# Other tick places for all pieces of a two-layer attention kernel, and layer 3's last transposes behind the next score

## The chip, the core and the metric

One core of one Trainium2 chip runs the whole kernel. The metric is device time in microseconds (us), taken from the first to the last instruction of the program with what lies around it.

## What is computed

32 batch elements, each a matrix x of 256 tokens by 256 features, go through four layers, cut here to what matters:

```python
# layer 0: conditioned norm over the whole matrix, twice, with two products
o = silu(scale * norm_all(x) + shift) @ W_in + b_in
x = silu(scale * norm_all(o) + shift) @ W_out + b_out + x
# layer 1: attention with 16 heads of 16, a bias of its own for each element and head, a mask
h = ln(x) * (1 + ada_scale) + ada_shift
s = einsum(q / 4, k) + attention_bias ; s[mask] = -inf
x = h + softmax(s) @ v @ Wo + bo
x = x + gelu2(ln(x) * g2 + beta2) @ W1 ... @ W2     # 256 -> 1024 -> 256
# layer 2: a small stencil on the matrix, coefficients from two grids
x = maximum(x + dt * (-grad(A x) + 0.5 * grad2(B x)), 0)
# layer 3: causal attention of 16 heads, then the 256 -> 1024 -> 256 block
x1 = x + causal_attention(ln(x)) @ Wo + bo
x2 = x1 + gelu(ln(x1) * gamma2 + beta2 ...) @ W2 + b2
out = x + gate * (x2 - x)
```

## The kernel before

The kernel is one long program without loops on the chip: the loops are unrolled when it is written. Work is cut into pieces with names (`score0`, `t4`, `w3` and so on), and time into ticks. Each element takes a PERIOD of 64 ticks. The layer-1 attention of element b starts at tick 64 b and its layer-3 attention at 64 b + 160 (`begin`, `S3`). An attention has 8 units of two heads, one each 4 ticks; in a steady period PE alternates between the 8 units of layer 1 of one element and the 8 of layer 3 of the element two before. A unit is called by its number, 0 to 7. The table `P` gives each piece its place in ticks from the begin of its element's layer (pieces named in `LATE` count from layer 3's), and `OWN` gives other places for the first two elements (0, 1) and the last two (-2, -1). `place` looks a place up, and from the places a table of what is due at each tick is made.

Each engine's program is written by one pass over the ticks: at each tick, first the attention pieces and then the others in the order in which the code has them. So a place only decides the order of instructions on their own engine; what makes an engine wait are semaphores. A smaller place is an earlier position in the queue, not an earlier time. Numbers that change without passing another piece of the same engine change nothing.

The queues and the pieces that the prediction speaks of:

- SyncE (SP) issues all loads. `ld_bt` (L396) loads the bias tile of a layer-1 unit into one of four BT buffers, after `v_bias` says that bias1 of the unit four before has been done. `stack` (L407 for Q, L411 for K) copies, for a pair of units, the rows of Q and K that its two scores need into Qs and Ks: three DMAs for Q and six for K, into one of two buffer sets. `ld_x`, `ld_xn` (L383), `ld_ab`, `ld_mask` (L390) load the element's inputs once each.
- TensorE (PE): `score0`, `score1` (L1191, wait for the stack's DMAs, `d_st`), `flip` (L1199, transposes of the exponentials), `pv` (L1217, L1218). For the tail of layer 3: `c3` (L1163, four transposes of the attention's result CX), `o3` (L1156, product with Wo), `t4` (L1163, four transposes of the normalised rows TC), `w3` (L1171, four groups of products with TN, the transposed rows), `w4`. Others are `wout` (L1156), `n2_ones` (L1263), `v3` (L1156) and so on.
- VectorE (DVE): `bias0`, `bias1` (L786, adds the bias tile and takes the row maximum), `low` (L794), `pvn` (L801 to L807, makes CX), `v3_out` (L867, reads v3's bank), `m4` (L945, and the statistics behind it), `f1` (L883), `n1_scale`, `n2_sum`, `n2_center`, `s_re`, `s_w`.
- ScalarE (ACT): `exp` (L990), `high` (L996), `c3_out` (L1088, copies c3's bank to TC), `m4_norm` (L1005, makes TC), `t4_out` (L1011, copies t4's bank to TN), `v1_mid`, `v1_hi`, `q1_out`, `t3_out`.
- GpSimd (POOL): `mask_add` (L497, adds the mask to the bias tile), `mask`, `y3`, `x1_bo`, `m1_b`, `q3_lo`, `k3_lo`.

c3, o3, t4, w3 of layer 3 and v3 of the next element share one PSUM bank, `bT_`, except for the last element. Therefore c3 of element b also waits for `v3_out` of element b + 1:

```python
for b in at(t, "c3"):
    ...
        T.wait_ge(v_v[3], b + 2)
```

The stack of unit 6 stands behind `ld_bt` of unit 7 in SP's queue. On PE, in a steady period around unit 6 of layer 1 of element 10, the order is: flips of unit 3, score1 of 5, pv of 2, `t4` of element 7, score0 of 6, flips of 4, `w3` group 0.

Of the kernel before, what the change touches and what calls it, by code (L numbers as in the profile page):

```python
# [42 lines left out]
def begin(layer, b):  # L43
# [6 lines left out]
    "score0": -2, "score1": 0, "bias0": 1, "bias1": 3, "exp0": 3, "exp1": 6, "flip0": 7, "flip1": 7,  # L50
    "high0": 8, "high1": 8, "low0": 10, "low1": 10, "pv0": 12, "pv1": 12, "pvn": 15,
    "ld_bt": -14, "mask_add": -9, "stack": -10,
    "ld_x": -103, "ld_xn": -34, "ld_ab": -34, "ld_mask": -109, "mask": -25,

# [7 lines left out]

# [2 lines left out]
    "s_pm": 74, "s_b": 82, "s_r": 74, "s_rp": 79, "s_re": 91, "s_ha": 83, "s_w": 91, "s_ab": 92, "s_row": 92,  # L65
    "s_mm": 95, "s_f": 104,

    "ld_w1": -24, "ld_sten": -46, "ld_w3": -277, "coefs": -21,

    "film_a": -72, "film": -62, "adas": -57, "scr": -48,  # L70

# [28 lines left out]
    },  # L100
# [5 lines left out]
        "s_b": 91, "s_r": 85, "s_rp": 86, "s_ha": 93, "s_w": 93, "s_ab": 93, "s_row": 93, "s_f": 98, "m3": -54,  # L106
# [4 lines left out]
    },  # L111
# [1329 lines left out]
```

## Time and profile before

| what | us |
|---|---|
| median of 3 runs | 2738.4 (2736.6 to 2738.7) |
| the profiled execution | 2738.3 |
| its span | 2737.0 |

Busy time in the span: PE 2599.0 (95%), ACT 2338.8 (85%), DVE 2221.9 (81%), PE's weight loads 2214.0 (81%, beside its matmuls), POOL 1674.0 (61%). The granted TensorE clock has a mean of 0.984 of full speed. The chain that ended last is 71% PE and 13% ACT. An engine's row in the timeline gives start, duration, line, operation, out<-in, the number of instructions in the row, and in brackets how long the engine had stood idle before it and what released it.

### The profile page before, as it was taken

To read this page: it belongs to the slowest core of one execution; us is meant where nothing else is said; L and a number is where in the kernel's file an instruction comes from. 1 tells how busy PE (TensorE), PEld (TensorE's weight loads), DVE (VectorE), ACT (ScalarE), POOL (GpSimd) and SP (SyncE) were. 2 spreads that over 40 slices of the span, in tenths; PEclk is the share of its full clock that TensorE was granted. 3 is DMA by queue.
4 is the path that set the end of the run, shared out by engine and by line. 5 is a ranking of instruction groups with operands and counts; after the bars stand their busy time and mean duration, and the time that the engine had idled before them with its cause. 6 is when DMAs were issued, how large, how long until landed. Compare 5 with 4: busy or idle time off the path is not lost.

```text
span 2737.0 us, 62626 instructions
## 1 busy us (share of the span) xinstructions
PE 2599.0 (95%) x20072; PEld 2214.0 (81%) x20072; DVE 2221.9 (81%) x7925; ACT 2338.8 (85%) x5285; POOL 1674.0 (61%) x1742
## 2 busy tenths in 40 slices
PE   8888999999999999999999999999999999999987
PEld 7766888888888888888888888888888888888776
DVE  5668888888888888888888888888888888888753
ACT  1567899999999999998999989999998998999865
POOL 2666666766667675666666566666666666765431
PEclk8988999999999999999999999999999999999999
DMA  6433343333333333333333333343333333333211
GB/s 230 130 96 102 91 118 108 116 102 113 96 103 115 109 114 103 110 98 101 114 112 112 103 108 101 98 119 108 113 97 114 101 100 116 109 105 102 63 31 29
DMA packets 176549, 287.96 MB, mean 105 GB/s; under 512 B 45856, under 2 KB 99104, under 8 KB 175840
## 3 DMA queue, kind: packets, MB, share of 16 engines
q1 hardware_dynamic: 176224, 283.97, 35.2%
q8 instruction: 162, 2.65, 0.4%
q14 instruction: 163, 1.34, 0.2%
HBM read 174.64 MB, written 8.45 MB: 67 GB/s over the span
## 4 chain that ended last, share of the span: by engine, by line
PE 71%; ACT 13%; issue 4%; SPq 4%; DVE 3%; POOL 2%; DMA 2%; ACTq 0%; DVEq 0%; POOLq 0%
PE bank L1171 15%; PE bank L1178 14%; PE bank L1199 10%; PE bank L1156 9%; PE bank L1148 8%; PE bank L1191 5%; ACT PB L990 3%; PE bank L1163 3%; SPq L411 2%; ACT PH L996 2%; PE bank L1306 2%; ACT BB L1011 2%; PE bank L1217 2%; PE bank L1218 2%; ACT AA L1011 2%
## 5 line engine op out<-in xcount | busy, mean ns | idle before, releaser
L990 ACT ACTIVATE PB<-PB,mx 128x256 f32<-128x256 f32 (+1 forms) x2048 | 834.6, 475 | 6.0 <-DVE mx L786 5.2
L794 DVE TENSOR_TENSOR PO<-bank,PH 128x384 f16<-128x384 f32 (+1 forms) x1024 | 589.4, 616 | 247.5 <-ACT PH L996 244.4
L497 POOL TENSOR_TENSOR BT<-BT,MN 128x1024 f32<-128x1024 f32 x256 | 545.9, 2137 | 174.2 <-DMA BT<-in_bias 173.4
L996 ACT ACTIVATE PH<-bank 128x384 f16<-128x384 f32 (+1 forms) x1024 | 499.0, 538 | 127.7 <-PE bank L1199 127.2
L1191 PE MATMUL bank<-Ks,Qs 96*128 96x512 f32 (+1 forms) x1024 | 519.1, 510 | 19.5 <-DMA Ks<-KU 11.9
L1199 PE MATMUL bank<-ident,PB 128*128 128x128 f32 x3584 | 484.8, 275 | 8.5 <-ACT PB L990 4.5
L1199 PEld LDWEIGHTS bank<-ident,PB 128*128 128x128 f32 x3584 | 421.2, 142 | 46.8 <-ACT PB L990 12.3
L786 DVE CUSTOM_DVE_ANT_0 PB<-bank,BT 128x256 f32<-128x256 f32 x1024 | 386.7, 416 | 37.6 <-PE bank L1191 36.2
L786 DVE CUSTOM_DVE_ANT_0 PB<-bank,caus 128x128 f32<-128x128 f32 (+1 forms) x1024 | 321.0, 351 | 22.9 <-PE bank L1191 22.5
L1217 PEld LDWEIGHTS bank<-VP,PH 128*128 128x128 f16 x3584 | 204.0, 96 | 119.2 <-issue 93.5
L1171 PE MATMUL bank<-TN,Wf 128*128 128x256 f32 x1024 | 253.9, 391 | 16.6 <-ACT BB L1011 11.4
L1171 PE MATMUL bank<-MB,Wf 128*128 128x256 f32 x1024 | 251.9, 389 | 14.2 <-ACT AA L1011 13.0
L1217 PE MATMUL bank<-VP,PH 128*128 128x49 bf16 x3584 | 257.5, 186 | 7.8 <-DVE CX L807 2.7
L1218 PE MATMUL bank<-VP,PO 128*128 128x49 bf16 x3584 | 249.7, 184 | 0.0
L1178 PE MATMUL bank<-Wf,BB 128*128 128x256 f32 x1024 | 244.8, 384 | 0.7 <-ACT BB L1000 0.7
L1178 PE MATMUL bank<-Wf,AA 128*128 128x256 f32 x1024 | 239.3, 381 | 1.6 <-ACT AA L1076 1.6
L1191 PEld LDWEIGHTS bank<-Ks,Qs 96*128 96x128 f32 x1024 | 195.1, 191 | 41.2 <-DMA Ks<-KU 16.0
L1171 PEld LDWEIGHTS bank<-TN,Wf 128*128 128x128 f32 x1024 | 184.9, 190 | 51.5 <-ACT BB L1011 21.0
L1171 PEld LDWEIGHTS bank<-MB,Wf 128*128 128x128 f32 x1024 | 184.2, 190 | 45.7 <-ACT AA L1011 24.0
L1178 PEld LDWEIGHTS bank<-Wf,AA 128*128 128x128 f32 x1024 | 189.4, 190 | 27.0 <-issue 2.1
L1218 PEld LDWEIGHTS bank<-VP,PO 128*128 128x128 f16 x3584 | 207.9, 97 | 0.7
L1178 PEld LDWEIGHTS bank<-Wf,BB 128*128 128x128 f32 x1024 | 185.2, 190 | 22.2 <-issue 1.0
(225 smaller groups left out, 5208.8 us busy)
## 6 DMA issues: line engine op xcount, KB each, us to landing
BT<-in_bias SPq DMA_DIRECT2D x256, 512.0 KB, 3.9
Qs<-QH SPq DMA_DIRECT2D x512, 64.0 KB, 2.4
Ks<-KH SPq DMA_DIRECT2D x1024, 32.0 KB, 2.0
Qs<-QU SPq DMA_DIRECT2D x256, 64.0 KB, 2.5
Ks<-KU SPq DMA_DIRECT2D x512, 32.0 KB, 2.0
XT<-in_xT SPq DMA_DIRECT2D x32, 256.0 KB, 2.9
X<-in_x SPq DMA_DIRECT2D x32, 256.0 KB, 2.9
AB<-ada_rows SPq DMA_DIRECT2D x32, 256.0 KB, 3.6
```

The lines of the kernel that those rows point to most:

```text
L497: G.op.tensor_tensor(v2(BT[k % 4]), v2(BT[k % 4]), MN[:, :].unsqueeze(1).broadcast_to([128, 2, 512]), ALU.add).then_inc(g_bt, 1)
L786: V.op.tensor_tensor_reduce(PB[(2 * D + q) % 6][:, h * 256:h * 256 + w], bS[q][:, h * w:h * w + w], plus, -1.0, 3.0e38, ALU.add, ALU.min, ...
L794: V.op.tensor_tensor(PO[i][:, 0:w], bP[h][:, 0:w], PH[i][:, 0:w], ALU.subtract).then_inc(v_low, 1)
L990: S.op.activation(o, o, ACT.Exp, scale=-1.0, bias=mx[u.layer][:, c:c + 1]).then_inc(a_exp, 1)
L996: S.op.activation(PH[i][:, 0:w], bP[h][:, 0:w], ACT.Copy).then_inc(a_high, 1)
L1156: last = T.op.matmul(half(ps, m), x[:, k * 256 + m * 128:k * 256 + m * 128 + 128], Wf[:, a + k * 256:a + k * 256 + 256], start=(k == 0), s ...
L1171: last = T.op.matmul(half(ps, f), Wf[:, c:c + 128], half(x, d), start=(d == 0), stop=(d == 1))
L1178: last = T.op.matmul(half(ps, q), x[:, f * 256 + q * 128:f * 256 + q * 128 + 128], Wf[:, c:c + 256], start=(g == 0 and f == 0 and q == 0), ...
L1191: T.op.matmul(bS[q][:, 0:2 * w].rearrange("p (h k) -> p h k", h=2), Qs[i][0:96, et * 256 + q * 128:et * 256 + q * 128 + 128], k2[:, :, 0:w ...
L1199: last = T.op.transpose(bP[h][:, c * 128:c * 128 + 128], PB[(2 * u.D + q) % 6][:, h * 256 + k * 128:h * 256 + k * 128 + 128], ident[:, :])
L1217: T.op.matmul(bV[:, o:o + 49], PH[i][:, c * 128:c * 128 + 128], vv, start=(n == 0), stop=False)
L1218: last = T.op.matmul(bV[:, o:o + 49], PO[i][:, c * 128:c * 128 + 128], vv, start=False, stop=(n == len(ks) - 1))
```

## The change

Only numbers in `P` and `OWN` change; each piece issues the same instructions as before. In steady periods `t4` moves from tick 53 to 54 of layer 3, which puts it behind `score0` of unit 6 of the layer-1 attention that runs beside it. `c3` moves from 45 to 43, ahead of score1 and the pv pair of the tick before. The rest of the table changes by small amounts, with `ld_xn`, `ld_mask`, `mask`, `ld_bt` and `stack` among them, and the places of the first two and the last two elements by larger ones. The diff, with `OWN` cut to lines that hold pieces spoken of:

```diff
--- before.py
+++ after.py
@@ -47,32 +47,32 @@
 
 
 P = {
-    "score0": -2, "score1": 0, "bias0": 1, "bias1": 3, "exp0": 3, "exp1": 6, "flip0": 7, "flip1": 7,
+    "score0": -2, "score1": 0, "bias0": 0, "bias1": 3, "exp0": 3, "exp1": 6, "flip0": 7, "flip1": 7,
     "high0": 8, "high1": 8, "low0": 10, "low1": 10, "pv0": 12, "pv1": 12, "pvn": 15,
-    "ld_bt": -14, "mask_add": -9, "stack": -10,
-    "ld_x": -103, "ld_xn": -34, "ld_ab": -34, "ld_mask": -109, "mask": -25,
-
-    "n1_stats": -81, "n1_ones": -68, "n1_sum": -66, "n1_center": -65, "n1_rstd": -66, "n1_scale": -60,
+    "ld_bt": -9, "mask_add": -7, "stack": -3,
+    "ld_x": -102, "ld_xn": -60, "ld_ab": -35, "ld_mask": -118, "mask": -7,
+
+    "n1_stats": -82, "n1_ones": -68, "n1_sum": -66, "n1_center": -65, "n1_rstd": -66, "n1_scale": -63,
     "n1_tanh": -58, "n1_gate": -56, "win": -49, "win_out": -45,
-    "n2_stats": -39, "n2_ones": -39, "n2_sum": -38, "n2_center": -36, "n2_rstd": -36, "n2_scale": -34,
-    "n2_tanh": -31, "n2_gate": -31, "xb": -33, "wout": -30, "x1": -28, "x1_rstd": -25, "x1_norm": -25,
-    "ada": -23, "t1": -21, "t1_out": -20, "x1_bo": -3, "q1": -19, "q1_out": -17, "q1_lo": -13,
-    "k1": -17, "k1_out": -13, "k1_lo": -10, "v1": -13, "v1_out": -9, "v1_hi": -5, "v1_sub": 7, "v1_mid": 8,
-    "v1_lo": 10,
-
-    "c1": 44, "c1_out": 45, "o1": 45, "m1": 47, "m1_rstd": 47, "m1_norm": 53, "m1_b": 71, "t2": 54, "t2_out": 54,
-    "w1": 57, "w1_out": 58, "w1_gelu": 66, "w2": 68, "f1": 74,
-    "s_pm": 74, "s_b": 82, "s_r": 74, "s_rp": 79, "s_re": 91, "s_ha": 83, "s_w": 91, "s_ab": 92, "s_row": 92,
-    "s_mm": 95, "s_f": 104,
-
-    "ld_w1": -24, "ld_sten": -46, "ld_w3": -277, "coefs": -21,
-
-    "film_a": -72, "film": -62, "adas": -57, "scr": -48,
-
-    "m3": -41, "m3_rstd": -41, "m3_norm": -35, "t3": -34, "t3_out": -33, "y3": -25, "q3": -30, "q3_out": -25,
-    "q3_lo": -24, "k3": -25, "k3_out": -24, "k3_lo": -14, "v3": -22, "v3_out": -19, "v3_hi": -4, "v3_sub": 1,
-    "v3_mid": 9, "v3_lo": 10, "c3": 45, "c3_out": 45, "o3": 46, "m4": 49, "m4_rstd": 50, "m4_norm": 52, "m4_b": 65,
-    "t4": 53, "t4_out": 54, "w3": 55, "w3_out": 57, "w3_gelu": 67, "w4": 69, "out": 75, "st_out": 77,
+    "n2_stats": -40, "n2_ones": -39, "n2_sum": -36, "n2_center": -36, "n2_rstd": -35, "n2_scale": -34,
+    "n2_tanh": -31, "n2_gate": -31, "xb": -30, "wout": -30, "x1": -29, "x1_rstd": -26, "x1_norm": -25,
+    "ada": -23, "t1": -21, "t1_out": -20, "x1_bo": -18, "q1": -19, "q1_out": -18, "q1_lo": -14,
+    "k1": -17, "k1_out": -13, "k1_lo": -8, "v1": -13, "v1_out": -9, "v1_hi": -4, "v1_sub": -3, "v1_mid": 3,
+    "v1_lo": 9,
+
+    "c1": 44, "c1_out": 45, "o1": 45, "m1": 47, "m1_rstd": 48, "m1_norm": 52, "m1_b": 64, "t2": 54, "t2_out": 54,
+    "w1": 57, "w1_out": 58, "w1_gelu": 66, "w2": 68, "f1": 73,
+    "s_pm": 74, "s_b": 81, "s_r": 74, "s_rp": 79, "s_re": 88, "s_ha": 87, "s_w": 89, "s_ab": 91, "s_row": 93,
+    "s_mm": 95, "s_f": 103,
+
+    "ld_w1": -32, "ld_sten": -56, "ld_w3": -164, "coefs": -31,
+
+    "film_a": -81, "film": -65, "adas": -62, "scr": -60,
+
+    "m3": -39, "m3_rstd": -37, "m3_norm": -36, "t3": -34, "t3_out": -34, "y3": -26, "q3": -30, "q3_out": -25,
+    "q3_lo": -18, "k3": -25, "k3_out": -24, "k3_lo": -18, "v3": -22, "v3_out": -19, "v3_hi": -3, "v3_sub": 1,
+    "v3_mid": 11, "v3_lo": 13, "c3": 43, "c3_out": 45, "o3": 46, "m4": 48, "m4_rstd": 52, "m4_norm": 52, "m4_b": 72,
+    "t4": 54, "t4_out": 54, "w3": 55, "w3_out": 57, "w3_gelu": 67, "w4": 69, "out": 75, "st_out": 79,
 }
 
 LATE = {
@@ -90,54 +90,56 @@
 OWN = {
     -2: {
...
-        "y3": -29, "q3": -41, "q3_out": -37, "q3_lo": -32, "k3": -37, "k3_out": -36, "k3_lo": -30, "v3": -29,
-        "v3_out": -22, "v3_hi": -22, "v3_sub": -21, "v3_mid": -16, "v3_lo": -14, "c3": 51, "c3_out": 112, "o3": 121,
-        "m4": 141, "m4_rstd": 145, "m4_norm": 150, "m4_b": 282, "t4": 153, "t4_out": 155, "w3": 159, "w3_out": 162,
+        "y3": -42, "q3": -45, "q3_out": -41, "q3_lo": -31, "k3": -38, "k3_out": -38, "k3_lo": -23, "v3": -37,
+        "v3_out": -23, "v3_hi": -19, "v3_sub": -19, "v3_mid": -17, "v3_lo": -16, "c3": 36, "c3_out": 137, "o3": 151,
+        "m4": 157, "m4_rstd": 167, "m4_norm": 171, "m4_b": 268, "t4": 175, "t4_out": 177, "w3": 196, "w3_out": 197,
...
     -1: {
...
-        "pvn_3": 110, "stack_3": 611, "c1": 43, "c1_out": 46, "o1": 47, "m1": 50, "m1_rstd": 51, "m1_norm": 55,
+        "pv1_3": 114, "pvn_3": 118, "stack_3": 608, "c1": 45, "o1": 47, "m1": 51, "m1_rstd": 52, "m1_norm": 56,
-        "t4": 578, "t4_out": 635, "w3": 638, "w3_out": 742, "w3_gelu": 910, "w4": 653, "out": 885, "st_out": 1135,
+        "m4_b": 575, "t4": 545, "t4_out": 574, "w3": 659, "w3_out": 769, "w3_gelu": 901, "w4": 733, "out": 965,
...
     0: {
...
-        "n2_rstd": -39, "n2_scale": -39, "n2_tanh": -39, "n2_gate": -38, "xb": -67, "wout": -33, "x1": -33,
+        "n1_gate": -54, "win": -51, "win_out": -50, "n2_stats": -48, "n2_ones": -48, "n2_sum": -44, "n2_center": -42,
-        "v3_sub": 0, "v3_mid": 4, "c3": 44, "m4": 47, "m4_rstd": 47, "t4": 54, "w3_gelu": 66, "out": 76, "st_out": 84,
+        "v3_mid": 2, "v3_lo": 10, "c3_out": 44, "m4": 49, "out": 76, "st_out": 89,
...
     1: {
...
-        "mask_add_1": 1, "stack_1": -13, "stack_3": -9, "ld_x": -72, "ld_xn": -57, "ld_ab": -28, "ld_mask": -62,
-        "n2_tanh": -33, "n2_gate": -33, "xb": -29, "x1_rstd": -26, "x1_norm": -24, "ada": -21, "t1": -18,
+        "mask_add_1": -5, "stack_1": -11, "stack_3": -5, "ld_x": -64, "ld_xn": -43, "ld_ab": -44, "ld_mask": -88,
+        "win_out": -53, "n2_stats": -52, "n2_ones": -51, "n2_sum": -49, "n2_center": -43, "n2_rstd": -49,
+        "n2_scale": -40, "n2_tanh": -37, "n2_gate": -35, "xb": -40, "wout": -35, "x1": -32, "x1_rstd": -30,
...
```

## Rows read from the trace of the kernel before

**Rows 1.** The page's busy times by engine.

```profile
PE 2599.0 (95%) x20072; PEld 2214.0 (81%) x20072; DVE 2221.9 (81%) x7925; ACT 2338.8 (85%) x5285; POOL 1674.0 (61%) x1742
```

**Rows 2.** Stretches: length; PE, PEld, DVE, ACT, POOL busy; clock; DMA share; GB/s.

```profile
859.40:939.40 80.00, 77.87 (x614) 66.59 (x613) 68.46 (x248) 72.78 (x166) 52.21 (x55) 1.00 0.36 107
1259.20:1340.80 81.60, 78.09 (x614) 66.69 (x613) 68.75 (x248) 72.92 (x166) 51.93 (x55) 1.00 0.36 105
```

**Rows 3.** PE's waits, 400 to 2400 us: us, times, longest.

```profile
PE bank L1163 <- ACT TC L1005: 20.6, 25, 1.1
PE bank L1156 <- ACT TC L1088: 11.3, 25, 0.5
...
PE bank L1191 <- DMA Ks<-KU: 2.7, 6, 1.4
```

**Rows 4.** Timeline of DVE, one steady period: v3_out, second half of bias1.

```profile
856.71 0.69 DVE L867 TENSOR_TENSOR HB<-bank,rows 128x512 f32<-128x512 f32 x1
...
858.99 0.42 DVE L786 CUSTOM_DVE_ANT_0 PB<-bank,BT 128x256 f32<-128x256 f32 x1
```

**Rows 5.** Timeline of SP, same period: ld_bt 7, first and last of the stack.

```profile
859.44 0.33 SPq L396 DMA_DIRECT2D BT<-in_bias  x1
859.82 0.57 SPq L407 DMA_DIRECT2D Qs<-QH  x1
...
864.29 1.23 SPq L411 DMA_DIRECT2D Ks<-KU  x2
```

**Rows 6.** All DMAs into Ks, from the view of that tile.

```profile
DMA to landing us min/median/max: 1.9/2.0/4.1
```

**Rows 7.** Timeline of PE, same period: c3, o3, t4, score0 of 6, flips, w3.

```profile
857.70 0.63 PE L1163 MATMUL bank<-ident,CX 128*128 128x128 f32 x4
...
859.02 1.99 PE L1156 MATMUL bank<-Wf,TC 128*128 128x256 f32 x8 [0.45 <-ACT TC L1088]
...
867.18 0.65 PE L1163 MATMUL bank<-ident,TC 128*128 128x128 f32 x4 [0.78 <-ACT TC L1005]
867.59 0.48 PE L1191 MATMUL bank<-Ks,Qs 96*128 96x512 f32 x1
867.90 1.04 PE L1199 MATMUL bank<-ident,PB 128*128 128x128 f32 x8
868.94 1.99 PE L1171 MATMUL bank<-TN,Wf 128*128 128x256 f32 x8
```

**Rows 8.** Timeline of ACT, same period: m4_norm and t4_out.

```profile
866.04 1.08 ACT L1005 ACTIVATE TC<-Y,smt 128x256 f32<-128x256 f32 x2
...
867.87 1.02 ACT L1011 ACTIVATE TN<-bank,cols 128x256 f32<-128x256 f32 x2
```

**Rows 9.** Timeline of SP, period from 1259.20: a long issue in the stack.

```profile
1260.24 2.80 SPq L407 DMA_DIRECT2D Qs<-QU  x1
1263.09 0.59 SPq L407 DMA_DIRECT2D Qs<-QH  x1
```

**Rows 10.** Timeline of PE, the same late period: score0 of 6, then w3.

```profile
1269.01 0.51 PE L1191 MATMUL bank<-Ks,Qs 96*128 96x512 f32 x1 [1.36 <-DMA Ks<-KU]
...
1270.22 1.03 PE L1171 MATMUL bank<-TN,Wf 128*128 128x256 f32 x4
```

**Rows 11.** The page's DMA queues: instructions (packets, MB, share).

```profile
q8 instruction: 162, 2.65, 0.4%
```

**Rows 12.** The page's groups: busy, mean ns, idle before and its releaser.

```profile
L794 DVE TENSOR_TENSOR PO<-bank,PH 128x384 f16<-128x384 f32 (+1 forms) x1024 | 589.4, 616 | 247.5 <-ACT PH L996 244.4
L497 POOL TENSOR_TENSOR BT<-BT,MN 128x1024 f32<-128x1024 f32 x256 | 545.9, 2137 | 174.2 <-DMA BT<-in_bias 173.4
L996 ACT ACTIVATE PH<-bank 128x384 f16<-128x384 f32 (+1 forms) x1024 | 499.0, 538 | 127.7 <-PE bank L1199 127.2
```

**Rows 13.** Timeline of PE near the start: the largest wait.

```profile
166.32 2.93 PE L1156 MATMUL bank<-Wf,FU 128*128 128x256 f32 x6 [4.12 <-DVE FU L758]
```

**Rows 14.** Timeline of PE near the end: w3 of element 30, a score.

```profile
2671.50 1.99 PE L1171 MATMUL bank<-TN,Wf 128*128 128x256 f32 x8 [1.11 <-ACT TN L1011]
...
2693.18 0.39 PE L1191 MATMUL bank<-Ks,Qs 96*128 96x256 f32 x1 [1.20 <-DMA Ks<-KU]
```

More of the change, by code:

```diff
@@ L92 @@
     -2: {
[7 rows of a table removed]
[7 rows of a table added]
     },
     -1: {
[4 rows of a table removed]
-        "s_b": 91, "s_r": 85, "s_rp": 86, "s_ha": 93, "s_w": 93, "s_ab": 93, "s_row": 93, "s_f": 98, "m3": -54,
[4 rows of a table removed]
-    },
[11 rows of a table removed]
-        "s_b": 88, "s_r": 88, "s_rp": 90, "s_re": 95, "s_ha": 95, "s_w": 96, "s_ab": 97, "s_row": 98, "s_mm": 100,
[3 rows of a table removed]
-    },
-    1: {
-        "score0_1": 1, "score1_1": 3, "bias0_1": 3, "exp0_1": 6, "flip0_1": 11, "flip1_1": 11, "high0_1": 12,
-        "high1_1": 12, "low0_1": 14, "low0_3": 9, "low1_1": 14, "pv0_1": 15, "pv1_1": 15, "pvn_1": 18, "ld_bt_1": -16,
-        "mask_add_1": 1, "stack_1": -13, "stack_3": -9, "ld_x": -72, "ld_xn": -57, "ld_ab": -28, "ld_mask": -62,
[6 rows of a table removed]
-        "s_r": 80, "s_rp": 88, "s_ha": 97, "s_w": 100, "s_ab": 101, "s_row": 106, "s_mm": 106, "s_f": 108,
-        "m3_rstd": -35, "y3": 0, "q3_lo": -25, "k3_out": -23, "k3_lo": -7, "v3_hi": -19, "v3_sub": -18, "v3_mid": -14,
-        "v3_lo": -10, "m4_b": 71, "out": 77,
[4 rows of a table added]
+        "s_b": 94, "s_r": 87, "s_rp": 88, "s_re": 94, "s_ha": 94, "s_w": 94, "s_ab": 94, "s_row": 94, "s_f": 101,
[4 rows of a table added]
+        "st_out": 1032,
+    },
+    0: {
+        "score0_1": 1, "score1_1": 3, "bias0_1": 4, "bias1_1": 5, "exp0_1": 5, "exp1_1": 7, "flip0_1": 8,
+        "flip1_1": 8, "high1_1": 10, "low0_1": 11, "low1_1": 11, "ld_bt_1": -3, "mask_add_1": 1, "stack_1": 4,
+        "stack_3": -1, "ld_x": -322, "ld_xn": -41, "ld_ab": -56, "ld_mask": -57, "mask": -39, "n1_stats": -219,
[7 rows of a table added]
+        "s_r": 82, "s_rp": 83, "s_re": 93, "s_ha": 96, "s_w": 97, "s_ab": 97, "s_row": 100, "s_mm": 100, "s_f": 108,
[3 rows of a table added]
+    },
+    1: {
+        "score1_1": -1, "bias0_1": 2, "bias0_3": 1, "exp0_1": 6, "flip0_1": 8, "flip1_1": 8, "high0_1": 11,
+        "high1_1": 12, "low0_1": 12, "low1_1": 12, "pv0_1": 14, "pv1_1": 14, "pvn_1": 18, "ld_bt_1": -18,
+        "mask_add_1": -5, "stack_1": -11, "stack_3": -5, "ld_x": -64, "ld_xn": -43, "ld_ab": -44, "ld_mask": -88,
[7 rows of a table added]
+        "s_w": 97, "s_ab": 99, "s_row": 104, "s_mm": 104, "s_f": 107, "m3": -51, "y3": 22, "q3_lo": -21, "k3_lo": -17,
+        "v3_out": -21, "v3_hi": -14, "v3_sub": -13, "v3_mid": -5, "v3_lo": 12, "m4_b": 68, "w3_gelu": 66, "out": 77,
+        "st_out": 83,
     },
```

49 rows, old and new, of the table OWN are left out of this document.

## The prediction

> **What bounds the kernel now.** I read the page first for the busiest engine: TensorE (PE) is busy for 2599.0 of 2737.0 us, and no other engine comes near [rows 1]. So the time is PE's own work plus the holes in it, and only an edit that changes the holes can change the time, since no instruction is added or removed. The table by stretches says where the holes are: a normal period of one batch element (80 us) has 77.87 us of PE, while one that starts at 1259.20 takes 81.6 us with 78.09 us of it [rows 2]. About 28 of the 32 periods (elements 3 to 30) are of this kind. Then PE's waits between 400 and 2400 us, 25 periods: two waits come once in every period, 20.6 us in all ahead of t4 (L1163, for m4_norm on ACT) and 11.3 us ahead of o3 (L1156, for c3_out on ACT); third, a wait in some periods only, 2.7 us in 6 times, where a score (L1191) waits for the DMAs of its stack [rows 3]. The change moves exactly t4 and c3, so these are read in the timeline.
>
> Times in a period are told from A, the end of bias1 of unit 3 of the layer-1 element on DVE, 858.99 + 0.42 = 859.41 in the period shown [rows 4]. On it hangs SP: ld_bt of unit 7 waits for that bias1 (it goes out at 859.44), and the nine DMAs of the stack of units 6 and 7 stand behind it on SP, 859.82 to 865.52 [rows 5]. From issue to landing such a DMA takes 1.9/2.0/4.1 us (min, median, max) [rows 6]; the last one goes out at about 864.9, so the stack lands at 866.94, which is A+7.52 and what the landing events show in 12 of the 28 periods within 0.05 us.
>
> In the period shown PE has finished the pv pair of unit 2 at 866.40, waits 0.78 us for m4_norm, does t4 at 867.18, score0 of unit 6 at 867.59, eight flips from 867.90, and w3.0 at 868.94 [rows 7]. m4_norm ends at 866.04 + 1.08 = 867.12, t4_out at 867.87 + 1.02 = 868.89 [rows 8], so w3.0 starts right at the end of t4_out. It is important that the score did not wait: it came 0.65 us after its landing, because the wait of t4 had covered it.
>
> **The change, part one: t4 behind score0 of unit 6 (P: 53 to 54).** The thought behind such an order is that the score fills t4's wait. The score can't: PE is free at 866.40 but the stack lands only at 866.94, so the wait becomes one for the stack and stays 0.58 of the 0.78 us. From then on, with the differences of the starts in the rows: score0 at landing + 0.04 (866.98), t4 0.32 later (867.30; the step from score to the next transpose is 867.90 - 867.59 = 0.31), t4 lasts 0.66, t4_out starts 0.05 behind and lasts 1.02, and w3.0, which multiplies what t4_out wrote, starts 0.05 behind that: landing + 2.13 = 869.07 instead of 868.94. That is +0.13 us: t4 itself has been made 0.12 later, and PE, which now finishes the flips about 0.2 us early, waits for t4_out in front of w3.0. Everything behind w3.0 on PE (scores of unit 6 and 7, n2_ones, w3.1 to w3.3) waits with it, and there is nothing in the row of PE to win it back before the next A, as the period has only some 2 us of holes.
>
> The price is higher where the stack is late, and it is late often. In the period from 1259.20 one Q DMA of the stack takes 2.80 us to issue instead of 0.59 [rows 9], the landing comes at A+9.75, and the score waits 1.36 us; t4 was already done under the wait and w3.0 follows at 1270.22, which is landing + 1.25 [rows 10]. With t4 behind the score, t4 and t4_out come after the landing in a row, and w3.0 comes at landing + 2.13: +0.88 us. Such long issues coincide with packets of the instruction queue (162 in the execution, about one each 17 us [rows 11]), so they walk through the period. The Trainium skill ("Runtime: NRT & Kernel Launch", section Instruction fetch mechanics) says that crossing a block of instructions is mostly hidden; by it all stacks would land at A+7.52 and the price would be the small one in every period. The trace disagrees with 2.80 us where 0.59 is usual.
>
> I worked the same two sums for each of the 28 periods from its own rows: w3.0 of before against the later of landing + 2.13 and its PE order. Nine periods have landings from A+8.05 to A+9.75 that give 0.74 to 0.88 each (7.7 us together), six, most with landings from A+7.7 to A+8.0, give 0.3 to 0.6 (2.65 us), thirteen give -0.1 to 0.17 (0.9 us). Sum **+11.3 us**. If no stack were late it would be 28 x 0.13 = +3.6, if all rest were as bad as the nine, 28 x 0.6 = +17; I take 11.3, since the number of SP instructions in a period stays and only two loads move past the stack, so the late issues come as often as before. I assume that a delay of w3.0 reaches the end of the period 1:1: the period of 1259.20 is 1.65 us longer than 79.96, and its w3.0 is 1.47 us later than usual (A+11.01 for A+9.54).
>
> **Part two: c3 ahead of score1 and the pv pair (45 to 43).** In before c3 (857.70) lets c3_out end at 858.97 and o3 waits 0.45 us for it to 859.02 [rows 7]. With c3 earlier the 0.45 looks free, up to 28 x 0.45 = 12.6 us. But c3's bank is the one that v3 of the next element used, and c3 waits for its reader v3_out on DVE, which ends at 856.71 + 0.69 = 857.40 [rows 4]. So c3 starts at about 857.44 instead of 857.70, now holding back score1's successors and the pv pair behind it, which takes the place of the wait: c3_out ends 0.26 earlier, and o3 follows the c3, pv pair and score0 issued behind it (1.27 us in all) at about 858.99. Gain 0.03 us a period, and even that is lost in the wait for the stack at A+7.52, because A (and so the stack) comes from score1 before it. I put 0 (bounds -0.45 and +0.05 a period).
>
> **Part three: the other steady places.** On DVE, n1_scale, f1, n2_sum, n2_center, s_re and s_w move by a few pieces; the cover is the idle time ahead of low, 247.5 us over the span for 1024 of them. On ACT, q1_out, v1_hi, v1_mid, t3_out move; the cover is 127.7 us ahead of high. On POOL, the mask goes right ahead of the first mask_add, and y3, x1_bo, m1_b, q3_lo, k3_lo change places; the cover is 174.2 us in which mask_add waits for bias DMAs [rows 12]. Worst single case: v1_mid ahead of a high adds 0.7 us on ACT where the next flips leave about 0.2; if it reached PE it would be +0.5 a period, but PE has a score and pv pair to do in between. On SP, ld_xn passes four stacks (1 DMA), ld_mask comes between two ld_bt, ld_x and ld_ab come ahead of the first stack of layer 3, and the stacks wait in place for their queues (default -10 to -3, ld_bt -14 to -9): the order of ld_bt 7 and stack 6 is unchanged, and the other stacks have 1.4 to 6 us between landing and score. Taken as 0; if one cover is gone, +0.1 to +0.3 us a period, and one that is removed may give back as much.
>
> **Part four: the ends.** The largest hole of PE in the first 330 us is 4.12 us ahead of wout of an early element [rows 13]. The new places put other pieces ahead of such waits and start the first stacks earlier. I can't follow it exactly; -2 us (bounds -6 and +3). At the end, w3 of element 30 (behind a wait of 1.11 us at 2671.50) moves from a hole between scores to the tail, up to 4 x 1.99 us of PE, while the stacks of the last units come some 2.8 us earlier and take away waits such as 1.20 us at 2693.18 [rows 14]. The tail had only about 3 us of idle PE to take it: +1 us (bounds -2 and +3).
>
> **Sum.** Profiled execution 2738.3 us (its span is 2737.0; the median 2738.4 is the same): 2738.3 + 11.3 + 0 + 0 - 2 + 1 = 2748.6; against the median, **2748.5 us**, +0.4%.
>
> **Rivals.**
> (1) Faster: the moves do what they are for. Condition: the landing of the stack is not what PE waits for, that is, SP sends it 0.5 us earlier or more (A less tied to the stack than I read). Then o3's 0.45 is won in each period and t4 costs nothing: w3.0 stays tied to t4_out. 28 x 0.45 = 12.6: 2738.3 - 12.6 - 1 = 2725. Against it: landing at A+7.52 in 12 periods, PE free at A+6.99, and v3_out for c3. It decides where the landing comes before A+7.0. Chance 0.10.
> (2) The late landings become rare, because ld_xn and ld_mask in front shift where the long SP issues fall: 2738.3 + 3.6 - 1 = 2741, the same as before. It is also what the page's rule named above would give, were it right. The trace speaks for about the same number. 0.17.
> (3) The change does nothing that PE feels: t4's place is made good before the next A, and ends cancel: 2738. For it, PE's 2 us of holes a period; against, the long period at 1259.20. 0.10.
> (4) A hidden move loses its cover: 0.25 us in each of 28 periods on top, 2755.5. 0.10.
> (5) The ends give 6 us or more and late landings get rare: 2732. 0.05.
> Forecast (2743.9 to 2753): 0.48.
>
> **How the numbers follow.** A difference of 0.2% (5.5 us) is about what a measurement tells from none. Faster than 2732.9: rival 1 and most of 5, 0.14. Within: rivals 2 and 3 and a tail of the forecast, 0.29. Slower than 2743.9: the forecast and rival 4, 0.57. Range: without rival 1 and the outer half of 4 and 5, 2734 to 2757. The forecast's own range is 2743 to 2753.
>
> **What would show it.** In the trace after: PE's wait ahead of t4 gone, and waits of a score for the stack in nearly every period, about 0.58 us each and some 25 x 0.9 in all in the steady part; a wait of 0.1 to 0.9 us ahead of w3.0 for t4_out (TN); c3 waiting for v3_out and o3's wait nearly gone but A and landing still 7.5 us apart; period 80.1 us instead of 79.96 and long ones 0.9 us longer. Wrong would make it: a stack landing before A+7.0, w3.0 at A+9.5 in periods with late stacks, or another hole in the period closing by as much as w3.0 is late.

## The result and the profile after

The changed kernel takes 2754.8 us (median of 4 runs, 2748.7 to 2762.2) against 2737.6 for before (a fourth run, of 2736.9, beside the three in the table above): ratio 1.0069, 95% interval 1.0044 to 1.0094, so 17 us slower. The prediction was 2748.5, range 2734 to 2757, slower with 0.57; the narrower range of the forecast alone, 2743 to 2753, is missed by 2 us. In the experiments below, one of the five runs of "t4 alone", 2806.1 us at a mean clock of 0.933, is in a slower state of the chip and is left out of its ratio. Its profiled execution is the longest of the four (2762.2, span 2760.9), so that the sums below, taken from it, come to 24 us and not to 17.

First the busy times of the changed kernel from its page, beside [rows 1]:

```profile
PE 2624.0 (95%) x20072; PEld 2236.5 (81%) x20072; DVE 2215.0 (80%) x7925; ACT 2342.4 (85%) x5285; POOL 1699.4 (62%) x1742
```

PE has the same 20072 matmuls as before and is busy 25.0 us longer. More waiting can't do that: the matmuls themselves ran slower in places. This already contradicts the prediction's first paragraph, by which only the holes in PE's row could change the time. The stretches tell where (length; PE, PEld, DVE, ACT, POOL busy; granted clock; DMA share; GB/s). The three cuts are the same points of both programs: up to A of element 3, from there to A of element 31, the rest. A is, as in the prediction, the end of bias1 of unit 3. Kernel before:

```profile
0.00:297.20 297.20, 252.18 (x1764) 212.10 (x1765) 200.48 (x667) 170.96 (x369) 166.37 (x166) 0.90 0.43 138
297.20:2544.30 2247.10, 2181.70 (x17136) 1864.65 (x17135) 1913.35 (x6853) 2036.99 (x4619) 1455.88 (x1511) 1.00 0.37 107
2544.30:2737.00 192.70, 165.09 (x1175) 137.29 (x1173) 108.07 (x411) 130.87 (x301) 51.75 (x66) 0.95 0.14 36
```

Changed kernel:

```profile
0.00:292.90 292.90, 250.04 (x1768) 212.10 (x1769) 199.72 (x667) 171.24 (x369) 168.17 (x166) 0.91 0.44 141
292.90:2565.90 2273.00, 2205.59 (x17135) 1885.72 (x17134) 1905.92 (x6851) 2040.61 (x4620) 1480.17 (x1512) 0.99 0.36 105
2565.90:2761.00 195.10, 168.32 (x1173) 138.72 (x1171) 109.39 (x409) 130.51 (x299) 51.09 (x66) 0.92 0.14 36
```

The start won 4.3 us, the 28 steady periods lost 25.9 (23.9 of them are longer busy time of PE, 2.0 are waits), the end lost 2.4 (3.2 more busy time, 0.8 less waiting). PE's waits between 400 and 2400 us, beside [rows 3] (two more lines in `OWN` have moved all line numbers by 2: the score is L1193, t4 and c3 are L1165, w3 is L1173):

```profile
PE bank L1193 <- DMA Ks<-KU: 26.0, 23, 1.9
PE bank L1219 <- DVE CX L809: 8.7, 24, 0.4
...
PE bank L1173 <- ACT TN L1013: 2.1, 9, 0.2
```

The waits of t4 for m4_norm (20.6 us) and of o3 for c3_out (11.3) are gone. In the place of the first stand 26.0 us in which a score waits for its stack, and in the place of the second 8.7 us of pv. A typical period, with A at 693.42, on PE (score0 of unit 6, t4, flips, w3.0), beside [rows 7]:

```profile
701.01 0.50 PE L1193 MATMUL bank<-Ks,Qs 96*128 96x512 f32 x1 [0.59 <-DMA Ks<-KU]
701.35 0.60 PE L1165 MATMUL bank<-ident,TC 128*128 128x128 f32 x4
701.78 1.04 PE L1201 MATMUL bank<-ident,PB 128*128 128x128 f32 x8
703.06 1.99 PE L1173 MATMUL bank<-TN,Wf 128*128 128x256 f32 x8 [0.24 <-ACT TN L1013]
```

and on ACT (m4_norm, t4_out), beside [rows 8]:

```profile
699.67 1.09 ACT L1007 ACTIVATE TC<-Y,smt 128x256 f32<-128x256 f32 x2
...
701.98 1.02 ACT L1013 ACTIVATE TN<-bank,cols 128x256 f32<-128x256 f32 x2 [0.42 <-PE bank L1165]
```

TC has been ready since 700.76, and yet t4 goes out at 701.35: it stands behind the score, and the score behind the landing at 700.96, which is A+7.54. On SP nothing has changed in order (ld_bt 7 right after A, the stack behind it), beside [rows 5]:

```profile
693.46 0.33 SPq L398 DMA_DIRECT2D BT<-in_bias  x1
693.83 0.57 SPq L409 DMA_DIRECT2D Qs<-QH  x1
...
698.31 1.24 SPq L413 DMA_DIRECT2D Ks<-KU  x2
```

What I had not foreseen is in other periods. Here is the same place in the period with A at 1016.69, where the stack came 0.5 us later:

```profile
1024.78 0.66 PE L1193 MATMUL bank<-Ks,Qs 96*128 96x512 f32 x1 [1.10 <-DMA Ks<-KU]
1025.24 1.05 PE L1165 MATMUL bank<-ident,TC 128*128 128x128 f32 x4
1026.09 1.91 PE L1201 MATMUL bank<-ident,PB 128*128 128x128 f32 x8
1027.79 2.18 PE L1173 MATMUL bank<-TN,Wf 128*128 128x256 f32 x8
```

Eight flips take 1.91 us instead of 1.04. The granted clock fell, right behind the wait of 1.10 us, from 2.4 to 1.2 GHz, for a stretch of 3.4 us. The profiled execution has 15 such stretches in its steady part, each within about 1 us of the end of the wait ahead of score0 of unit 6, where before has one. The period of 1016.69 is 81.7 us long with 79.39 us of PE, while a typical one has 77.94 of 80:

```profile
693.40:773.40 80.00, 77.94 (x613) 66.56 (x612) 67.95 (x248) 72.86 (x166) 52.82 (x55) 1.00 0.37 107
1016.70:1098.40 81.70, 79.39 (x613) 68.05 (x612) 68.18 (x246) 72.88 (x166) 52.84 (x55) 0.98 0.36 105
```

### The profile page after: what moved, and what is told of

The parts are those of the page before. It is cut to its first block, busy times and chain, and to the rows that moved or that the text cites. A ratio compares the mean times of both kernels' runs of the same rounds, so it can differ in the third digit from the quotient of the medians.

```text
span 2760.9 us, 62627 instructions
## 1 busy us (share of the span) xinstructions
PE 2624.0 (95%) x20072; PEld 2236.5 (81%) x20072; DVE 2215.0 (80%) x7925; ACT 2342.4 (85%) x5285; POOL 1699.4 (62%) x1742
## 4 chain that ended last, share of the span: by engine, by line
PE 71%; ACT 10%; SPq 7%; DVE 5%; issue 4%; DMA 3%; POOL 1%; ACTq 0%; DVEq 0%; POOLq 0%
PE bank L1173 16%; PE bank L1180 16%; PE bank L1201 10%; PE bank L1158 8%; PE bank L1150 8%; PE bank L1193 5%; SPq L413 4%; PE bank L1165 3%; DMA Ks<-KU 3%; SPq L409 2%; ACT PB L992 2%; PE bank L1308 2%; ACT BB L1013 2%; ACT PH L998 2%; PE bank L1219 2%
## 5 line engine op out<-in xcount | busy, mean ns | idle before, releaser
L1193 PE MATMUL bank<-Ks,Qs 96*128 96x512 f32 (+1 forms) x1024 | 523.6, 514 | 45.7 <-DMA Ks<-KU 37.8
L1201 PE MATMUL bank<-ident,PB 128*128 128x128 f32 x3584 | 500.0, 281 | 14.5 <-DVE PO L796 8.5
L1201 PEld LDWEIGHTS bank<-ident,PB 128*128 128x128 f32 x3584 | 431.3, 145 | 54.7 <-ACT PB L992 22.1
L1173 PE MATMUL bank<-TN,Wf 128*128 128x256 f32 x1024 | 259.7, 398 | 17.6 <-ACT BB L1013 10.4
L1173 PE MATMUL bank<-MB,Wf 128*128 128x256 f32 x1024 | 251.9, 389 | 15.3 <-ACT AA L1013 13.0
L1193 PEld LDWEIGHTS bank<-Ks,Qs 96*128 96x128 f32 x1024 | 195.0, 191 | 72.3 <-DMA Ks<-KU 45.8
L1173 PEld LDWEIGHTS bank<-TN,Wf 128*128 128x128 f32 x1024 | 191.2, 197 | 51.8 <-ACT BB L1013 19.2
L1173 PEld LDWEIGHTS bank<-MB,Wf 128*128 128x128 f32 x1024 | 184.2, 190 | 46.8 <-ACT AA L1013 23.7
```

Source lines behind the costliest of these rows:

```text
L1173: last = T.op.matmul(half(ps, f), Wf[:, c:c + 128], half(x, d), start=(d == 0), stop=(d == 1))
L1193: T.op.matmul(bS[q][:, 0:2 * w].rearrange("p (h k) -> p h k", h=2), Qs[i][0:96, et * 256 + q * 128:et * 256 + q * 128 + 128], k2[:, :, 0:w ...
L1201: last = T.op.transpose(bP[h][:, c * 128:c * 128 + 128], PB[(2 * u.D + q) % 6][:, h * 256 + k * 128:h * 256 + k * 128 + 128], ident[:, :])
```

## The experiments

The number in brackets behind a time is the ratio to before with its 95% interval. "Steady part" is A of element 3 to A of element 31 in the profiled execution: 2247.1 us for before, 2273.0 for the changed kernel.

### t4 alone

```diff
-    "t4": 53,
+    "t4": 54,
```

In the kernel before. 

> The kernel before with one number changed: t4 at 54, behind score0 of unit 6. My theory (the score cannot fill t4's wait, since the stack lands after PE is free, and t4 then stands behind the landing; where the stall is long, PE's granted clock falls to half for 3.4 us, which costs about 1.3 us more): nearly the whole loss of the changed kernel, 2748 to 2758 us, with a wait of about 0.6 us or more ahead of score0 of unit 6 in each of the 28 steady periods. Rival (the loss is c3's, which puts score1 and so bias1 and the stack 0.24 us later): 2739 to 2743 us and hardly a low clock. Rival 3 (the loss comes from the other places): 2738 to 2740 us.

Measured: 2751.2 us (1.0059, 1.0045 to 1.0073), steady part 2257.8. The first theory holds: t4's place alone makes the kernel slower by 14 us, without c3 and the other places. PE's waits, 400 to 2400 us:

```profile
PE bank L1191 <- DMA Ks<-KU: 25.2, 24, 1.8
PE bank L1156 <- ACT TC L1088: 11.3, 25, 0.5
...
PE bank L1171 <- ACT TN L1011: 5.2, 22, 0.2
```

Against [rows 3] t4's 20.6 us have become 25.2 us for the stack and 5.2 us ahead of w3. The steady part is 10.7 us longer than that of before, where the prediction's sum for this part was 11.3, and only two of the 28 periods have a low clock (one in before). The rest of the 14 us lies mostly in the end, 195.0 us instead of 192.7.

### c3 alone

```diff
-    "c3": 45,
+    "c3": 43,
```

In the kernel before. 

> The kernel before with one number changed: c3 at 43, ahead of score1 and the pv pair. My theory: o3's wait of 0.45 us goes and the same 0.2 to 0.3 us come back where c3 pushes score1 and bias1, on which the stack of unit 6 hangs; the period stays within 0.1 us of 79.95 and late landings cost a little more: 2736 to 2743 us. Rival (c3 is what made the score wait): 2747 us or more. Rival (it wins the 0.45 us of each period): 2726 to 2730 us.

Measured: 2738.0 us (1.0003, 0.9993 to 1.0013). Typical periods are 79.78 us instead of 79.95. PE's waits, 400 to 2400 us:

```profile
PE bank L1163 <- ACT TC L1005: 17.8, 25, 1.3
...
PE bank L1163 <- DVE HB L867: 8.1, 25, 0.3
PE bank L1217 <- DVE CX L807: 7.1, 25, 0.4
...
PE bank L1191 <- DMA Ks<-KU: 2.0, 5, 0.6
```

The wait for v3_out that the prediction named stands there, 0.3 us in each period. o3's 11.3 us are gone. In the period with A at 1179.77:

```profile
1179.35 1.89 PE L1156 MATMUL bank<-Wf,TC 128*128 128x256 f32 x8
```

o3 starts only 0.03 us earlier against A than in [rows 7], as forecast, but it no longer stands behind a wait and takes 1.89 us instead of 1.99, so it ends 0.13 us earlier, and m4_norm follows. What comes out is 0.17 us a period in the typical ones, which would be 4.8 us in 28. The profiled execution shows 1.7 us of it (steady part 2245.4), as it has three low-clock stretches, after stalls of the score up to 0.6 us, and before has one; its start and end are 2.1 and 4.8 us longer than those of before, and it is one of the slowest of eleven runs (2733.1 to 2744.9). So c3 alone is a small gain at most, which the measurement doesn't tell from none.

### All of the change but t4

```diff
-    "t4": 54,
+    "t4": 53,
```

In the changed kernel. 

> The changed kernel with t4 put back to 53, all else as changed. My theory: the time falls back to that of before or a little under, since the first 293 us had won 4.4 us and the end lost 2.4: 2733 to 2742 us, and no or few stretches of low clock between 300 and 2400 us. Rival (c3 or the other places carry the loss): 2747 us or more.

Measured: **2727.2 us** (0.9966, 0.9954 to 0.9979), 10 us faster than before and 28 us faster than the changed kernel. This was better than I expected. Start and end gained (292.9 and 190.0 us instead of 297.2 and 192.7), and the steady part is 2239.1, 8.0 us under before, with typical periods of 79.56; these sums are from the profiled execution, the fastest of the five (2723.2). PE's waits, 400 to 2400 us:

```profile
PE bank L1165 <- ACT TC L1007: 10.2, 25, 0.8
PE bank L1219 <- DVE CX L809: 9.1, 25, 0.4
...
PE bank L1193 <- DMA Ks<-KU: 6.0, 11, 1.3
```

The wait ahead of t4 is half of that in [rows 3], since m4_norm ends earlier. The place, in the period with A at 691.67:

```profile
699.04 0.66 PE L1165 MATMUL bank<-ident,TC 128*128 128x128 f32 x4 [0.39 <-ACT TC L1007]
699.46 0.50 PE L1193 MATMUL bank<-Ks,Qs 96*128 96x512 f32 x1
699.80 1.04 PE L1201 MATMUL bank<-ident,PB 128*128 128x128 f32 x8
700.81 2.00 PE L1173 MATMUL bank<-TN,Wf 128*128 128x256 f32 x8
```

Here t4 (A+7.37) still goes out before the stack lands (A+7.75 in this period, A+7.54 in the usual ones), and w3.0 starts at A+9.14.

### The changed default places with the old ends

```diff
 OWN = {
...
```

The changed kernel with the whole table `OWN` of before. 

> The changed kernel with the table OWN of before, so only the default places are changed and the first two and last two elements have the places of before (those that OWN names). My theory: the loss stays, since it lies in the steady periods, and the 2 us net that the ends gave are lost: 2750 to 2762 us. Rival (the ends interact with the steady loss, by shifting where the long SP issues fall): 2740 to 2747 us.

Measured: 2782.8 us (1.0171, 1.0157 to 1.0185). The steady part is 2274.5, within 2 us of the changed kernel's, but the start takes 305.8 us (292.9), the end 201.1 (195.1), and the steady part includes a first period of 85.7. Neither theory foresaw that. The places of the first and last elements are made for the default places beside which they run; the two parts can't be judged apart, and the 4.3 us won at the start need both. The run does confirm that most of the steady loss doesn't come from the ends: the 27 periods behind the first are 22.9 us longer than those of before, where the changed kernel's are 26.8 longer.

### The stack ahead of every odd ld_bt

```diff
-    "ld_bt": -14,
+    "ld_bt": -13,
```

In the kernel before. 

> The kernel before with ld_bt at -13, which on SP puts the stack of units 6 and 7 ahead of ld_bt of unit 7 (and each other stack ahead of the odd ld_bt beside it). The stack then no longer waits for bias1 of unit 3 and should land about 2 us earlier against PE's stream. My theory: only the waits for late stacks go (about 5 us in 28 periods), the period stays near 79.95, as m4_norm sets t4: 2730 to 2735 us. Rival (the loads of the bias tiles, now 5.7 us later, make mask_add and then bias late): 2740 us or more.

Measured: 2750.5 us (1.0063, 1.0041 to 1.0086); the rival's number, but only half its reason. The stack now lands at A+4.9 to A+6.3 and no score waits for it. The steady part is 2247.6, nothing won and nothing lost: m4_norm still sets t4, and other periods became longer by as much as the late ones gained. The loss is in the start, 309.3 instead of 297.2 us.

```diff
-    "ld_bt": -9,
+    "ld_bt": -6,
```

The same order in the changed kernel. 

> The changed kernel, t4 at 54 kept, with ld_bt at -6, so that the stack of units 6 and 7 stands ahead of ld_bt of unit 7. My theory (t4 behind the score costs because the stack lands after PE is free): with the stack there in time, score0 waits no more, t4 waits shortly for m4_norm, the low clocks of the steady part go, and the time falls from 2755 to that of the changed kernel with t4 back or less: 2718 to 2730 us. Rival (t4 behind the score costs in itself, through t4_out and w3.0): 2740 us or more.

And with t4 back at 53. 

> The changed kernel with t4 back at 53 and ld_bt at -6: the same order on SP as in the run above, only t4 ahead of the score. My theory: the waits for late stacks go (6 us in the steady part of the kernel with t4 back), 2718 to 2726 us; beside the run above it tells what t4's place is worth once the stack is early: within 4 us of it. Rival (t4's place matters whatever the stack does): over 8 us under the run above.

Measured: 2874.6 us (1.0504, 1.0488 to 1.0520) and 2869.0 us (1.0491, 1.0476 to 1.0507). Both of my theories fall. PE's waits of the first, 400 to 2400 us:

```profile
PE bank L1201 <- DVE PO L796: 60.2, 47, 2.5
PE bank L1219 <- DVE CX L809: 15.6, 43, 0.4
...
PE bank L1193 <- DMA Ks<-KU: 0.4, 2, 0.2
```

The score's wait is gone as meant (0.4 us), but flips wait 60.2 us for low on DVE. The later bias tiles hold up mask_add on GpSimd, behind which n1_rstd and n2_rstd stand, and those hold up DVE. The edit moved too many loads at once to test what I wanted. Only this much can be read: between t4 at 54 and at 53 there are 5.5 us with the stack early, which lies between my "within 4" and the rival's "over 8".

### The stack ahead of one ld_bt

```diff
+            late = 3 if piece in ("ld_bt", "mask_add") and u.layer == 1 and u.n == 7 and 3 <= u.b <= 29 else 0
-            due[piece].setdefault(starts[u.D][0] + place(piece, u.b, NB, f"_{u.layer}"), []).append(u)
+            due[piece].setdefault(starts[u.D][0] + place(piece, u.b, NB, f"_{u.layer}") + late, []).append(u)
```

So only ld_bt and mask_add of unit 7 move, in steady elements. In the changed kernel. 

> The changed kernel (t4 at 54), and in elements 3 to 29 ld_bt of unit 7 alone 3 ticks later, so that SP issues the stack of units 6 and 7 ahead of it, and mask_add of unit 7 also 3 ticks later. The stack is then free of bias1 of unit 3. My theory: it lands before PE is free, score0 does not wait, the low clocks go, 2720 to 2732 us. Rival (the bias tile of unit 7, 5.7 us later, now makes bias0 of unit 7 or pieces behind it on GpSimd wait): 2745 us or more.

The same with t4 back at 53. 

> The same swap on SP and GpSimd in the changed kernel with t4 back at 53. My theory: against the kernel with t4 back alone (2727) the waits for late stacks go, 6 us and two low clocks: 2716 to 2725 us, and the run with t4 at 54 beside it within 4 us. Rival (the time is set by what stands behind, as it was when all odd loads moved): 2727 us or more.

Measured: **2719.8 us** (0.9931, 0.9908 to 0.9954) and **2720.4 us** (0.9933, 0.9907 to 0.9959). This is the test that settles the cause: the same place of t4 that costs 28 us with the stack at A+7.5 costs nothing measurable once the stack lands between A+5.6 and A+7.1: typical periods are 79.63 us with t4 behind the score and 79.56 with t4 ahead, which is 2 us in 28 periods and less than these runs can tell. The loss came neither from t4 nor from t4_out, but from what t4 was put behind. In the first, with A at 691.88:

```profile
699.07 0.48 PE L1194 MATMUL bank<-Ks,Qs 96*128 96x512 f32 x1 [0.20 <-DMA Ks<-KU]
699.39 0.60 PE L1166 MATMUL bank<-ident,TC 128*128 128x128 f32 x4
699.83 1.08 PE L1202 MATMUL bank<-ident,PB 128*128 128x128 f32 x8
701.10 1.99 PE L1174 MATMUL bank<-TN,Wf 128*128 128x256 f32 x8 [0.20 <-ACT TN L1014]
```

The score comes at A+7.2, and the wait of 0.20 us ahead of it is the same in nearly every period, wherever the stack lands between A+5.6 and A+7.1. So it is not the landing that ends it, though the trace puts it down to that here; over 400 to 2400 us the waits name another releaser in most periods:

```profile
PE bank L1194 <- DVE mx L789: 5.0, 23, 0.5
```

That is the bias add of the unit before, which has to be done with the score's bank (the score also waits for `v_bias`); in the period with A at 851.61 it ends at A+7.04. With the stack early, this is what bounds score0, and w3.0 starts at A+9.22. Even a long SP issue (here 1.84 us in the stack, landing A+7.13) is covered. Both kernels beat before by 17 us and the changed kernel by 35. The second one's steady part (2236.2) is 2.9 us under the one without the swap.

### The landing made later

```diff
+  if c == 0 and x == 1 and u.n == 6 and 3 <= u.b <= 30:
+      S.op.dma_start(Qb[0:16, :], src[32 * j:32 * j + 16, :]).then_inc(d_du, 16)
+      S.op.dma_start(Qb[16:32, :], src[32 * j + 16:32 * j + 32, :]).then_inc(d_st[J % 2], 16)
+      continue
```

In the kernel before (the score also waits for `d_du`). 

> The kernel before with a tenth DMA in the stack of units 6 and 7 (elements 3 to 30): its first Q copy is split in two halves of 16 rows, so SP issues 0.6 us longer and the stack lands at about A+8.1 instead of A+7.5 (A is the end of bias1 of unit 3). My theory (in before the wait of t4 for m4_norm covers the first 0.6 us): typical periods stay at 79.95, those with late stacks lose up to 0.6 us each: +3 to +9 us in 28 periods, 2740 to 2747 us, and a few low clocks. Rival (SP's own queue is the bound, so every period pays 0.6): 2753 us or more.

With t4 at 54. 

> The same dose in the kernel before with t4 at 54. My theory (with t4 behind the score nothing covers the landing): every steady period pays the 0.6 us, 17 us in all over the 2751 of t4 alone, and the stalls of 1.2 us or more bring low clocks in many periods, up to 1.3 us each: 2768 to 2790 us. Rival (the place of t4 costs a fixed amount whatever the landing): as much above t4 alone as the dose costs in before, under 2762 us.

Measured: 2753.4 us (1.0045, 1.0025 to 1.0066) and 2774.4 us (1.0128, 1.0091 to 1.0164). In typical periods the stack lands at A+8.17, 0.65 later. These periods say it in the plainest way: 79.94 us with t4 first (79.95 before), 80.66 with t4 behind (80.05 without the extra DMA). The lines of the score in period 13 of each, first t4 first, then t4 behind:

```profile
1107.41 0.50 PE L1198 MATMUL bank<-Ks,Qs 96*128 96x512 f32 x1
```

```profile
1111.51 0.50 PE L1198 MATMUL bank<-Ks,Qs 96*128 96x512 f32 x1 [1.22 <-DMA Ks<-KU]
```

The first kernel was over its forecast of 2740 to 2747: in elements 15 to 28 landings came at A+8.5 to A+9.6, and the cover of 0.6 us had been used up by the extra DMA. Its low clocks were four stretches. As recorded, the rival of a fixed cost of t4's place (under 2762) is out. But the dose cost 16 us in before where I had put 3 to 9; with that price a fixed cost would give 2767 us, which the four runs (2764.7 to 2781.1) don't exclude. What excludes it are the typical periods: t4's place costs 0.72 us there with the later landing and 0.10 without.

### The wait filled

```diff
+   if q == 0 and u.layer == 1 and u.n == 6 and 3 <= u.b <= 30:
+       T.wait_ge(v_t, 5 * (u.b - 3) + 1)
+       warm(4)
    T.wait_ge(d_st[i], stack_done(D))
```

In the changed kernel. 

> The changed kernel with four matmuls without use (128x128, into the bank that t4 writes next) ahead of score0 of unit 6 in elements 3 to 30, in the wait for the stack; they take about 0.5 us of it. Theory 1 (part of the loss is the granted clock that falls to half after a stall): the low-clock stretches of the steady part become rare, each worth about 1.3 us: 2738 to 2748 us. Theory 2 (the stretches come from something else than this hole): the same number of them and 2751 us or more.

Measured: 2749.6 us (1.0048, 1.0031 to 1.0065), four runs within 3.3 us where the changed kernel's four spread over 13.5. The steady part is 2263.1 instead of 2273.0, without a single low-clock stretch before element 31's period:

```profile
293.00:2556.20 2263.20, 2210.95 (x17359) 1888.52 (x17358) 1903.30 (x6853) 2040.70 (x4620) 1479.61 (x1512) 1.00 0.37 106
```

Theory 1 has its mechanism: the same waits for the stack (landings here were even later, up to A+9.05, with up to 1.1 us left of the wait) bring no low clock when PE works through the first half microsecond. The time lies just above its range. The four matmuls cost some 0.15 us where the stack is on time, but that holds for only five periods here; more weighs that 23 landings instead of 20 come at A+7.85 or later, and all 28 together are 6.4 us later than in the changed kernel. Why they are is not shown.

## Why the prediction was right, and where not

**t4 behind the score.** Right in mechanism and size, against the kernel before: forecast +11.3 us, measured with t4 alone 10.7 us in the steady part. The forecast of the single steps, w3.0 at landing + 2.13, measures landing + 2.10 (A+9.61 with the landing at A+7.51).

**c3 at 0.** Here the step failed. I wrote that c3 starts behind v3_out, which was right (0.33 us of wait with c3 alone), and so was the gain of 0.03 us at o3's start. But the term was put at 0 because the gain "is lost in the wait for the stack", and that holds only with t4 behind the score. With t4 first, o3's end is what counts: 0.13 to 0.15 us (c3 alone) or 0.38 us (with the rest) earlier against A, and m4_norm, t4 and w3.0 come forward by about the same. The reason that I gave, that A comes from score1, doesn't fit the trace either: A comes 2.19 to 2.20 us behind the flips ahead of c3 in before, with c3 alone and in the changed kernel, for bias1 waits there for `low` on DVE and not for its score.

**The other steady places at 0.** Also off: with c3 they make typical periods 79.56 instead of 79.95. The trace shows where most of this enters: v3_out ends at A-2.25 instead of A-2.02, the flips ahead of c3 end at A-2.19 in both, so c3's wait of 0.33 us shrinks to 0.09 and o3 starts at A-0.66 (A-0.43 with c3 alone). Which of the changed places brings v3_out forward was not separated. All kernels follow one line, from A:

| kernel | m4_norm ends | stack lands | w3.0 starts | period |
|---|---|---|---|---|
| before | 7.71 | 7.53 | 9.54 | 79.95 |
| c3 alone | 7.55 | 7.50 | 9.37 | 79.78 |
| all but t4 | 7.33 | 7.54 | 9.14 | 79.56 |
| t4 alone | 7.71 | 7.52 | 9.61 | 80.05 |
| changed | 7.33 | 7.51 | 9.61 | 80.02 |
| changed, one swap | 7.32 | 5.9 to 7.1 | 9.22 | 79.63 |

With t4 first, w3.0 is m4_norm + 1.82 (and landing + 1.25, if that is later); with t4 behind, it is 2.0 to 2.05 behind score0, that is, landing + 2.10, or A+9.22 if the stack is early and the bias add bounds the score. The period follows w3.0 one to one. So the two parts of the change are not a sum: the rest had won 0.39 us a period, and t4's place, costing 0.10 in before, costs 0.46 there, since it puts w3.0 back on the landing. That is 13 of the 34 us between the steady parts of "all but t4" and "changed" (2239.1 and 2273.0). 13 more stretches of low clock make some 16, and the last 5 fit the late stacks, where the same place costs 0.85 us (landing + 2.10 for landing + 1.25).

**The clock, a term that was missing.** The prediction had no price for a low clock, and its first paragraph excluded one: only the holes were to change the time, but PE's busy time rose by 25.0 us. In the changed kernel, periods with a wait of about 1.1 us ahead of the score are 80.5 to 80.65 us long without a low stretch (two cases) and 81.7 with one (four cases): 1.2 us each, some 18 us for 15 stretches in the profiled execution. Its four runs order themselves by this: 2748.7 and 2751.3 us at a mean clock of 0.983, 2758.3 at 0.978, 2762.2 at 0.975. The forecast of 2748.5 is met by the runs with the higher clock. Only the slowest of the four has a trace. An estimate: 0.983 instead of 0.975 is 22 us of full clock more over the span, and a stretch of 3.4 us at half the clock takes 1.7, so these two runs had some 13 stretches fewer; at 1.2 us each that is 16 us, and they are 11 to 13 us faster.

**Start and end.** Forecast -2 and +1, measured -4.3 and +2.4, inside the bounds. The end's +1 was for work of w3 moved there. What is measured is another thing: PE waits 0.8 us less there, but 30.7 us of the end run at 1.2 GHz instead of 20.5; with t4 back at 53 it is 17.1 us, and the end takes 190.0.

**Late stacks.** Rival 2 had them rare. By the Trainium skill ("Runtime: NRT & Kernel Launch", section Instruction fetch mechanics), which calls the crossing of a block of instructions mostly hidden, they would be rare too. The trace disagrees again: 20 of the 28 landings of the changed kernel come at A+7.85 or later, 14 in before, mostly because one issue in the stack takes 0.8 to 1.7 us. **Rival 1** (faster, if the landing comes before A+7.0) gave 2725 and the point from which it decides; with landings from A+5.6 to A+7.1 the changed kernel takes 2720. So the rival's condition was right, on another kernel. Its sum was not: it counted o3's 0.45 us in each period, and typical periods won 0.32 (79.95 to 79.63).

The right direction was no luck, the right range in part: the 8 us that the other places won in the steady part and the larger price of t4 beside them, with the clock, were both missing, and they pull in opposite directions.

## What to carry to other kernels

Before moving work behind an instruction to fill a wait, look up when that instruction's own input lands; a wait can be the cover of a second one that the trace doesn't show, as here t4's wait covered the stack's landing, and it is the later of the two that counts after the move. Two edits that act on the same maximum are not a sum: work out the point (here w3.0) as a maximum over both inputs, for each combination. If the landing is the later one, move the transfer first: one load out of its way was worth 35 us here, though moving all its fellows in the same way cost 120. And a wait on a busy engine may cost more than its length, if the clock falls behind it.

## What the runs showed of the hardware

The granted clock can fall around single waits of about a microsecond on an engine that is 95% busy. In the steady parts the stretches at 1.2 GHz lasted 3.4 us, sometimes 6.8, and each began within 1.5 us of a wait of PE. The length of the wait alone doesn't decide: in the changed kernel 0.97 us was followed by one (element 13), 1.16 and 1.32 us were not (elements 26 and 17), and in the kernel with t4 behind and the later landing six waits of 2.1 to 2.6 us passed without one and one of 2.5 us did not. What else must come together was not found. Half a microsecond of matmuls without use in the wait made them vanish in the steady part (15 to 0), with at most 1.1 us of wait left behind it.

PE also paid a little right behind a wait: o3's eight matmuls took 1.99 us there and 1.89 without a wait ahead of them, t4's four 0.65 and 0.60.
